# A graph network on one core: messages in four partition quarters of a PSUM bank, and a copy placed between two halves of a comparison

## The reference

```
W   = (edge_attr @ ew + eb).reshape(E, 16, 16)
msg = einsum('ei,eio->eo', h[src], W)
agg = segment_sum(msg, dst, num_segments=12500)
h   = agg + h @ rw + rb
```

## Time and profile before

| | |
|---|---|
| median of 3 runs | 7843.1 us (7841.94 to 7845.44) |
| the profiled execution | 7844.59 us, of which the span of its instructions is 7842.8 us |
| busy, share of the span | PE 94%, PEld 84%, DVE 75%, ACT 64%, POOL 68% |
| mean granted TensorE clock | 0.978 of full speed |
| picks, line 1074 | 30000 matmul records, 5729.9 us busy |
| gathers, line 468 | 5625, 5323.8 us busy |

### The profile page before, as it was taken

How to read it: one execution, slowest core, us unless ns; L and a number is a source line. 1 busy time by engine, 2 the same in 40 slices (tenths; PEclk the granted TensorE clock), 3 DMA queues, 4 the chain that set the end, 5 groups by cost and what they waited for, 6 DMA issues and landing times.

```text
span 7842.8 us, 135584 instructions
## 1 busy us (share of the span) xinstructions
PE 7377.1 (94%) x51692; PEld 6562.7 (84%) x51692; DVE 5875.9 (75%) x7566; ACT 5020.2 (64%) x8367; POOL 5324.6 (68%) x5635
## 2 busy tenths in 40 slices
PE   4999999999999899999999999999999999999998
PEld 2888888888888688888888888868888888888887
DVE  3777777777777677777777777767777777777775
ACT  3666666666666466666666666656666666666665
POOL 4677777777777377777777777737777777777772
PEclk7999999999999799999999999989999999999998
DMA  7111111111111111111111111111111111111110
GB/s 37 29 30 30 30 30 30 30 30 30 30 28 29 26 30 30 28 30 30 30 30 30 30 30 30 29 25 29 30 30 30 30 27 30 30 30 30 30 30 20
DMA packets 783265, 229.16 MB, mean 29 GB/s; under 512 B 643869, under 2 KB 733869, under 8 KB 782619
## 3 DMA queue, kind: packets, MB, share of 16 engines
q1 hardware_dynamic: 529252, 172.27, 10.7%
q0 software_dynamic: 180000, 46.44, 6.9%
q10 hardware_dynamic: 73367, 1.76, 1.0%
HBM read 216.52 MB, written 3.52 MB: 28 GB/s over the span
## 4 chain that ended last, share of the span: by engine, by line
PE 66%; ACT 28%; issue 2%; DVE 2%; DMA 1%; DVEq 1%; ACTq 0%
PE bank L1074 57%; ACT distance L914 13%; ACT low_hot L918 13%; PE bank L1088 2%; PE bank L1030 2%; PE bank L1089 2%; ACT z L878 1%; PE bank L1097 1%; PE bank L1098 1%; DMA key_all<-in_src 1%; PE bank L1143 1%; DVE xbig L638 1%; PE bank L1155 1%; DVEq L719 0%; DVE agg L724 0%
## 5 line engine op out<-in xcount | busy, mean ns | idle before, releaser
L468 POOL DMA_INDIRECT xg<-node_table,idx x5625 | 5323.8, 946 | 2394.5 <-issue 1768.1
L1074 PE MATMUL bank<-nodes,low_hot 128*128 128x400 f32 x30000 | 5729.9, 348 | 25.0 <-DVE nodes L651 15.1
L1074 PEld LDWEIGHTS bank<-nodes,low_hot 128*128 128x128 f32 x30000 | 5401.4, 188 | 285.0 <-issue 254.8
L914 ACT ACTIVATE distance<-key_all,low_id 128x640 bf16<-128x640 int16 x3000 | 2242.6, 818 | 2056.8 <-issue 1298.9
L683 DVE TENSOR_TENSOR spread<-mask,bank 128x400 f32<-128x400 uint8 x3750 | 2015.5, 565 | 1571.9 <-PE bank L1074 1571.6
L918 ACT ACTIVATE low_hot<-distance,one 128x640 fp32r<-128x640 bf16 x3000 | 2231.0, 815 | 0.0
L688 DVE TENSOR_REDUCE xg<-spread 128x80 f32<-128x2000 f32 x750 | 1677.3, 2236 | 25.7
L638 DVE TENSOR_TENSOR xbig<-xg,bank 128x1280 f32<-128x1280 f32 x750 | 1327.4, 1810 | 1.0 <-issue 0.2
L1041 PE MATMUL bank<-xbig,hot 128*32 128x144 f32 x18750 | 992.6, 294 | 0.0
L1041 PEld LDWEIGHTS bank<-xbig,hot 128*32 128x32 f32 x18750 | 819.7, 109 | 163.6 <-issue 101.3
L1088 PEld LDWEIGHTS bank<-merge,z 128*128 128x128 f32 x942 | 146.7, 188 | 428.2 <-ACT z L878 422.8
(11 more groups left out here) (109 smaller groups left out, 1031.3 us busy)
## 6 DMA issues: line engine op xcount, KB each, us to landing
key_all<-edge_keys SPq DMA_DIRECT2D x375, 320.0 KB, 3.7
xg<-node_table,idx POOLq DMA_INDIRECT x5625
ea<-in_edge_attr SPq DMA_DIRECT2D x375, 100.0 KB
idx<-in_src SPq DMA_DIRECT2D x375, 7.5 KB
node_table<-rows_room SPq DMA_DIRECT2D x3, 781.2 KB
xbig<-node_table SPq DMA_DIRECT2D x9, 192.0 KB
xbig<-in_x SPq DMA_DIRECT2D x2, 781.2 KB
xbig<-in_dst ACTq DMA_DIRECT2D x1, 782.5 KB, 68.1
```

Source lines behind the costliest of these rows:

```text
L468: pool.indirect_dma_start(out=xg[u][:, j, :], out_offset=None, in_=table[:, :], in_offset=bass.IndirectOffsetOnAxis(ap=idx[u][:, j:j + 1], ...
L914: nc.scalar.activation(distance[f][:, 0:tiles.stop - tiles.start, :], key[u % KEYS][:, tiles, :], ACT.Abs, bias=low_id[:, f:f + 1]).then_i ...
L1074: last = nc.tensor.matmul(p_sel[t % BANKS], low_hot[:, f, t, :], nodes[i][:, f, :, :].rearrange("p d f -> p (d f)"), start=(f, i) == (0, 1 ...
```

## The change

`p_agg`, the place of the messages, becomes a list: rounds 0 to 3 of a group of five lie in the four partition quarters of bank 2 at columns 0 to 99, and round 4 in quarter 0 at columns 100 to 199. `messages_of` issues a matmul of 100 columns for each round: the four with `w_now`, then the four with `eb_now`, then the two of round 4. VectorE's adds read the new places.

In ScalarE's order, `copy_rounds(g)` moves from the head of slot g+1 into slot g: between the four distances and the four one-hots of half 1. In the last two slots of a layer, which have no comparison, it stands at the slot's end.

```
-        p_agg = bank[2][0:D, 0:QROUNDS * SPAN].rearrange("d (q w) -> d q w", w=SPAN)
+        p_agg = [bank[2][q % GANG * WIN:q % GANG * WIN + D, q // GANG * SPAN:(q // GANG + 1) * SPAN]
+                 for q in range(QROUNDS)]
...
-                    nc.vector.tensor_tensor(here, here, p_agg[:, r % QROUNDS, :], ALU.add).then_inc(s_add, 1)
+                    nc.vector.tensor_tensor(here, here, p_agg[r % QROUNDS], ALU.add).then_inc(s_add, 1)
...
-            def compare_keys(layer, b, u, half):
+            def compare_keys(layer, b, u, half, between=None):
...
+                if between is not None:
+                    copy_rounds(layer, between)
...
-                        if g:
-                            copy_rounds(layer, g - 1)
                         copy_picked_rows(layer, b, u)
...
                             compare_keys(layer, b, u + 2, 0)
-                            compare_keys(layer, b, u + 2, 1)
-                copy_rounds(layer, G - 1)
+                            compare_keys(layer, b, u + 2, 1, between=g)
+                        else:
+                            copy_rounds(layer, g)
...
-                to = p_agg[:, 0:count, :].rearrange("d q w -> d (q w)")
-                nc.tensor.matmul(to, w_now[:], zT[:, 0:count, :].rearrange("p q w -> p (q w)"), start=True, stop=False)
-                nc.tensor.matmul(to, eb_now[:], zxT[:, 0:count, :].rearrange("d q w -> d (q w)"),
-                                 start=False, stop=True).then_inc(s_mm, 1)
+                for first in range(0, count, GANG):
+                    some = range(first, min(first + GANG, count))
+                    for q in some:
+                        nc.tensor.matmul(p_agg[q], w_now[:], zT[:, q, :], start=True, stop=False)
+                    for q in some:
+                        last = nc.tensor.matmul(p_agg[q], eb_now[:], zxT[:, q, :], start=False, stop=True)
+                last.then_inc(s_mm, 1)
```

## The result

The changed kernel takes 7481.0 us (median of 4, 7477.7 to 7481.8), against 7842.5 us for the kernel before beside it (median of 4). The ratio is 0.9538, 95% interval 0.9522 to 0.9555: 361.5 us less. 7447 was predicted, from 7400 to 7535. A second session gave 7480.6 against 7843.5, ratio 0.9538 (0.9511 to 0.9566).

The account below looks back on a forecast made before the run. TensorE was taken to set the pace, its transposes waiting for ScalarE's copy `z`. Gains per layer of 67.4 + 40.2 + 0 + 24.5 = 132.1 us, 396 in three, gave 7447 us, range 7400 to 7535.

Parts of the forecast that it names:

- The copy's place: ScalarE's copy ahead of four one-hots ends the transposes' wait for `z`: 1.07 us gained per simple slot, 67.4 per layer.
- VectorE's hold: In the slot with adds, VectorE's late takes hold the fifth pick about 1.1 us; the slot keeps 19.19 us, gaining nothing.
- The rival without the hold: DVE does not hold the fifth pick: 96 us more, but POOL's pace then binds, about 7360 us; chance 0.04.
- The messages: Twenty 100-column records in four partition quarters run side by side: 1.08 us instead of 1.87, 0.79 gained, 24.5 per layer.
- the slow end: All ten message pairs go one after the other: 2.70 us per group of messages, a loss of 0.83.
- the slot with two rounds: Transposes start at T+5.57 instead of T+6.81, T being the sums' start: 1.34 us gained per slot, 40.2 per layer.
- POOL: Gather issue takes 18.73 us per slot against a new mean slot of 18.76; its lead is kept, so it does not bind.
- The messages in a row: Rival: message matmuls run serially, 2.70 us in place of 1.08, giving 7598 us, or 7520 halfway; chance 0.13 for both.
- another wait in place of `z`: Rival: the transposes wait as late for masks, previous copies or adds; about 7735 us, chance 0.04.
- a slower gather: Rival: denser DVE work holds up gather issues; at 1.35 us per gather about 7990 us, slower than before; chance 0.03.
- a binding POOL: Rival: gathered rows land later than thought, costing 20 to 30 us per layer, up to 7530 us; chance 0.08.

## Why the prediction was right, step by step

*The copy's place: right.* 1.07 us was predicted for a simple slot, and 1.06 measured (19.07 to 18.01), also with the copy's move alone. The cover behind it held: the one-hots never held a pick, and the copy was ready 2 us early.

*VectorE's hold: right.* The slot with the adds was to keep its 19.19 us; it has 19.2. Its transposes start at T+5.94 (3028.58), 0.6 us earlier than before, but the fifth pick at T+10.29 (3032.93), as late as before. Some 90 times the weights for this pick wait 0.85 us for a take, where 1 us was expected. One reading was off: VectorE's chain was not back to back from T, since 0.7 us before the adds it waits for their addresses. Moving the adds gave 117 us back, which confirms the cause. The rival without the hold was put at 96 us, cut by POOL's pace to about 7360; the run with the adds moved came out at 7363.7.

*The messages: right in kind and size.* 1.08 us predicted, 1.13 measured, 2.74 in one quarter (2.70 was the upper bound). The rule of the Trainium skill's "TensorE: Matmul & The Clock Gate" (Part 3: Packing small matmuls), that a weight load goes beside running matmuls only where the row group differs, would have given the slow end. The trace disagrees: four pairs with their weights in four quarters took 0.29 us.

*The term that was mis-sized: the slot with two rounds.* The prediction gave it 1.34 us for the wait, and with the messages 2.13. It gained 1.80 (21.82 to 20.02 us): 0.27 less on the wait, and 0.05 less on the messages. The one such slot I had read, 22.07 us long, was one of three; the other 87 take 21.80 to 21.83. Its transposes started at T+6.81. A typical one, from the timeline of PE before:

```profile
2829.49 2.64 PE L1041 MATMUL bank<-xbig,hot 128*32 128x144 f32 x50
...
2836.04 0.47 PE L1088 MATMUL bank<-merge,z 128*128 128x100 f32 x2 [0.79 <-ACT z L878]
...
2846.33 1.01 PE L1097 MATMUL bank<-zT,w_now 128*16 128x500 f32 x2
...
2848.21 3.19 PE L1074 MATMUL bank<-nodes,low_hot 128*128 128x400 f32 x16
2851.33 0.92 PE L1041 MATMUL bank<-xbig,hot 128*32 128x144 f32 x18
```

Here they start at T+6.55 like nearly all others, and the slot has 21.84 us. Going by the starts of the sums through both traces, four slots take 79.1 us before in most cases and not 79.4, and 75.25 after. So per layer 63 x 1.06 + 30 x 1.80 - 30 x 0.03 = 119.9 us, in three layers 360, against 361.5 measured; the 36 us between that and the 396 predicted are 90 x 0.33 = 30 for this slot, 2 for the last wide group of messages in each of the three layers, which stands in none of these slots, and the rest 0.01 to 0.03 us in each of the others. A group of rows that is to stand for thirty others should have been looked up in three of them.

*POOL: right.* The paces met at 18.76 and 18.73 us in the forecast; in fact the mean slot is 18.81, and no engine waited for gathers: their lead in the second layer grew from 36 us in the second slot to 45 in the last.

*The rivals.* The messages in a row, another wait in place of `z`, a slower gather (0.947 us each, gaps of 0.30, as before), and a binding POOL did not come. VectorE's hold was there. What the Trainium skill warns of in "SBUF — State Buffer" (Who interferes with whom) was not seen: the gathers kept their pace with VectorE 78% busy. No run here changed the modes in which VectorE's instructions run.

## What to carry to other kernels

When a wait in a steady loop goes, work out for each kind of slot what is next, from the waiting engine's own chain: here three kinds of slot gained 1.06, 1.80 and nothing, and the one that gained nothing named the next change, which was worth 117 us. Small matmuls that write 16 or 32 partitions ran side by side here once they lay in different partition quarters of the bank, and an engine's side work belongs where its trace shows it waiting, not at the end of its loop, where the next chain starts. Read a repeated pattern in several places before its number is multiplied by ninety.

## What the runs showed of the hardware that was not expected

In four of the seven sessions every kernel was slower by about a half, the kernel before among them (11.45 to 11.81 ms). They ran on three chips, one of which gave undisturbed times in another session. The trace of the copy alone (first run) shows where, in PE's timeline:

```profile
5016.80 1.11 PE L1042 MATMUL bank<-xbig,hot 128*32 128x144 f32 x19
5018.33 0.28 PE L1042 MATMUL bank<-xbig,hot 128*32 128x144 f32 x1 [0.42 <-issue]
5019.05 0.30 PE L1042 MATMUL bank<-xbig,hot 128*32 128x144 f32 x1 [0.43 <-issue]
...
5021.86 0.40 PE L1042 MATMUL bank<-xbig,hot 128*32 128x144 f32 x1 [1.79 <-issue]
```

The sums begin at full pace, and after 20 to 25 of their 50 records TensorE goes on one record in 0.7 us, or in 1.4 or 2.1, though the profile shows nothing that it waits for. In this trace 3119 of the 18750 records of the sums stand behind such a stop of over 0.2 us, and 3 of the 30000 of the picks, whose records are 0.19 us apart. In the run with the messages alone the stops also fell into the new messages (20 records in 1.13 us), in the ones with the copy moved as well they hardly did. The granted clock does not start it: it was 1.00 (full speed, 2.4 GHz) from 5016.80 to 5020.50, where the stops have begun, and 0.50 (1.2 GHz) from 5021.00 to 5027.50, behind them.

The stops keep company with the gathers. POOL is idle for over half of this trace, yet no stop in the sums starts more than 2.8 us behind the end of a gather. In each layer the first sum and the last four have no stops; the other 360 of the 375 sums do. At the first layer's end the gathers' last row on POOL, and the rows of the sums on PE from there on, are these:

```profile
4020.75 0.94 POOL L468 DMA_INDIRECT xg<-node_table,idx  x1 [0.30 <-issue]
```

```profile
4024.70 2.32 PE L1042 MATMUL bank<-xbig,hot 128*32 128x144 f32 x21 [0.30 <-issue]
...
4043.81 2.64 PE L1042 MATMUL bank<-xbig,hot 128*32 128x144 f32 x50
...
4061.82 2.64 PE L1042 MATMUL bank<-xbig,hot 128*32 128x144 f32 x50
```

From there on the slots are 18.01 us again. The stops also begin only when the gathers go on after their first five slots. A gather less per slot won 515 us in a disturbed session, which agrees. In such a session the copy's move made the kernel 4 to 5% slower and the messages alone 1.7%, where the two together gain 4.6% in an undisturbed one. No run tested what gathers and short matmuls have in common, or why some sessions have these stops and others none; the cause stays open.
